# Roots and reciprocals of a two-layer kernel moved to a power operation on GpSimd

## The reference

```python
def _layernorm(x, axis=-1, eps=1e-05):
    m = jnp.mean(x, axis=axis, keepdims=True)
    v = jnp.var(x, axis=axis, keepdims=True)
    return (x - m) / jnp.sqrt(v + eps)
...
xn = _layernorm(x, axis=-1)
x = x + attention0(xn) + experts(xn)     # distance attention: softmax(-sqrt(d2)); 7 experts and a shared one
xn = _layernorm(x, axis=-1)
x = x + attention1(xn) + ffn1(xn)        # dot-product attention
# ffn1:
real = jnp.einsum('bti,io->bto', x, jnp.cos(theta + theta_noise))
imag = jnp.einsum('bti,io->bto', x, jnp.sin(phi + phi_noise))
return jnp.sqrt(real * real + imag * imag)
```

## Time and profile before

| | |
|---|---|
| time, median of 2 runs | 1760.43 us (1755.08 and 1765.78) |
| span of the profiled execution | 1763.0 us |
| PE / DVE / ACT / POOL busy | 84% / 79% / 88% / 18% of the span |

### The profile page before, as it was taken

How to read it: one execution, slowest core, us unless ns; L and a number is a source line. 1 busy time by engine, 2 the same in 40 slices (tenths; PEclk the granted TensorE clock), 3 DMA queues, 4 the chain that set the end, 5 groups by cost and what they waited for, 6 DMA issues and landing times. The chain is left out here.

```text
span 1763.0 us, 25680 instructions
## 1 busy us (share of the span) xinstructions
PE 1483.9 (84%) x8038; PEld 490.8 (28%) x8039; DVE 1387.5 (79%) x1687; ACT 1547.0 (88%) x959; POOL 323.9 (18%) x239
## 2 busy tenths in 40 slices
PE   5737988998898888878888887476699999999997
PEld 3411233233323332332333223354211111111113
DVE  6658966977887788779877975278699999999996
ACT  3537997999999999999999999254699999999996
POOL 2310660221122022202220221353300000000000
PEclk9755978999999999999999989778655555555556
DMA  6781231011101110111011100384300000000001
GB/s 199 209 247 36 67 110 34 27 27 35 28 26 35 30 34 25 35 30 34 25 30 35 31 22 12 63 198 155 100 27 27 27 26 23 27 27 27 27 22 48
DMA packets 80328, 99.07 MB, mean 56 GB/s; under 512 B 23874, under 2 KB 52690, under 8 KB 80290
## 3 DMA queue, kind: packets, MB, share of 16 engines
q1 hardware_dynamic: 72162, 78.23, 15.3%
q0 software_dynamic: 8128, 20.36, 4.2%
HBM read 52.69 MB, written 45.88 MB: 56 GB/s over the span
## 5 line engine op out<-in xcount | busy, mean ns | idle before, releaser
L1129 DVE TENSOR_SCALAR scores<-ring 128x1024 f32<-128x1024 f32 x512 | 597.7, 1214 | 59.2 <-PE ring L930 59.0
L1468 PE MATMUL a_ring<-a_stk 72*128 72x512 bf16 x1024 | 480.8, 621 | 6.5 <-DMA a_stk<-stack 6.5
L1604 DVE TENSOR_REDUCE a_den<-a_exp 128x2 f32<-128x2048 f32 x192 | 426.3, 2278 | 36.3 <-ACT a_exp L1579 36.3
L1419 ACT ACTIVATE scores<-scores 128x8192 f32<-128x8192 f32 x64 | 446.3, 7020 | 0.2
L1412 ACT ACTIVATE scores<-scores 128x8192 f32<-128x8192 f32 x60 | 417.6, 7022 | 16.8 <-DVE scores L1129 16.6
L1579 ACT ACTIVATE a_exp<-a_ring 128x1024 f32<-128x1024 f32 x384 | 428.0, 2133 | 3.5 <-PE a_ring L1468 3.5
L942 PE MATMUL pvb<-scores,val 128*9 128x256 f32 x4096 | 325.4, 395 | 48.4 <-ACT scores L1419 39.1
L930 PE MATMUL ring<-stk 72*128 72x512 bf16 x1024 | 333.0, 411 | 27.2 <-DMA w<-in_w 17.1
L1581 ACT ACTIVATE a_ring<-a_ring 128x1024 f32<-128x1024 f32 x128 | 203.0, 2144 | 0.0
L1468 PEld LDWEIGHTS a_ring<-a_stk 72*128 72x128 bf16 x1024 | 69.8, 111 | 416.8 <-ACT a_exp L1579 287.2
L1581 ACT ACTIVATION_READ_ACCUMULATOR a_ring<-a_ring 128x1 f32 x128 | 143.6, 1314 | 0.0
(11 more groups left out here) (181 smaller groups left out, 1151.0 us busy)
## 6 DMA issues: line engine op xcount, KB each, us to landing
stk<-stack SPq DMA_DIRECT2D x64, 192.0 KB
a_stk<-stack SPq DMA_DIRECT2D x64, 192.0 KB, 2.8
stack<-qp SPq DMA_DIRECT2D x8, 768.0 KB, 3.5
stack<-kp SPq DMA_DIRECT2D x8, 768.0 KB, 4.2
xj<-xg SPq DMA_DIRECT2D x16, 320.0 KB, 3.3
yg<-ht POOLq DMA_DIRECT2D x16, 320.0 KB, 3.1
stack<-qp SPq DMA_DIRECT2D x8, 512.0 KB, 4.5
stack<-kp SPq DMA_DIRECT2D x8, 512.0 KB, 4.9
```

The costliest lines, as they stand in the source:

```text
L1129: nc.vector.tensor_scalar(S[place][:, j * N:(j + 1) * N], tile[:], 1e-12, None, ALU.max).then_inc(ring_free, 1)
L1419: nc.scalar.activation(S[place][:], S[place][:], ACT.Exp, scale=-1.0).then_inc(exp_done, 1)
L1468: mm = nc.tensor.matmul(out[:, cols], stk[place][:, Q, i * P:(i + 1) * P], stk[place][:, K, cols], start=True, stop=True)
L1604: nc.vector.tensor_reduce(den[side][:, h, 2 * pair:2 * pair + 2], E[pair][:], axis=AX, op=ALU.add).then_inc(summed, 1)
```

## The change

Both roots leave ACT and the reciprocal leaves DVE. Two constants, -0.5 and 0.5, stand in a tile `powers`. POOL raises the variance plus eps (128 x 8) to the power -0.5 in one instruction, which gives the reciprocal of the deviation, and the sums of squares (128 x 1024) to the power 0.5, which gives the magnitudes. Both are tensor-tensor operations with the exponent broadcast as the second operand. The new POOL steps are `deviations(b)`, which waits for `var_ready`, and `magnitudes(b)`, which waits for `pow_ready`. SP's and PE's programs are the same as before.

```diff
+    R["powers"] = sb("powers", [P, 2])
...
+            chain.step(nc.vector.memset(R["powers"][:, 0:1], -0.5))
+            chain.step(nc.vector.memset(R["powers"][:, 1:2], 0.5))
...
-            def magnitudes(b):
-                act.wait_ge(pow_ready, b + 1)
-                nc.scalar.activation(mag[:, :, :], mag[:, :, :], ACT.Sqrt).then_inc(mag_ready, 1)
-
-            def begin(b):
-                if not first and is_first(b):
-                    keep_attention(b)
-                act.wait_ge(var_ready, b + 1)
-                nc.scalar.activation(rstd[:], mv[:, :, 1], ACT.Sqrt).then_inc(std_ready, 1)
...
-                if not is_first(b):
-                    keep_sums(b - 1) if first else magnitudes(b - 1)
+                if first and not is_first(b):
+                    keep_sums(b - 1)
...
-                if first and not is_last(b):
-                    begin(b + 1)
...
-                    if not is_last(b):
-                        begin(b + 1)
...
+            def deviations(b):
+
+                pool.wait_ge(var_ready, b + 1)
+                nc.gpsimd.tensor_tensor(rstd[:], mv[:, :, 1], R["powers"][:, 0:1].to_broadcast([P, NT]),
+                                        ALU.pow).then_inc(std_ready, 1)
+
+            def magnitudes(b):
+                pool.wait_ge(pow_ready, b + 1)
+                flat = mag[:, :, :].rearrange("p t c -> p (t c)")
+                nc.gpsimd.tensor_tensor(flat, flat, R["powers"][:, 1:2].to_broadcast([P, N]),
+                                        ALU.pow).then_inc(mag_ready, 1)
+
             def batch(b):
                 if not first and not is_last(b):
                     begin(b + 1)
+                if not first and not is_first(b):
+                    magnitudes(b - 1)
+                if first and not is_last(b):
+                    deviations(b + 1)
 
                 pool.wait_ge(kp_ready, b)
                 pool.wait_ge(qk_f, 2 * b + 2)
                 nc.gpsimd.tensor_tensor(kr[:], kf[:], kp[:, 0, :], ALU.subtract).then_inc(kr_ready, 1)
                 pool.wait_ge(kp1_ready, b + 1)
                 nc.gpsimd.tensor_tensor(kp[:, 2, :], kr[:], kp[:, 1, :], ALU.subtract).then_inc(kp_ready, 1)
+                if not first and not is_last(b):
+                    deviations(b + 1)
...
                 begin(0)
+                deviations(0)
                 for b in range(B):
                     batch(b)
+                magnitudes(B - 1)
...
-                begins.step(nc.vector.reciprocal(rstd[:], rstd[:]))
-                begins.wait()
```

More of the change, by code:

```diff
@@ L487, in batch @@
                                              ).then_inc(mix_out, 1)
-                    if not is_last(b):
-                        begin(b + 1)
-            each_batch(act, batch, begin)
-            keep_sums(B - 1) if first else magnitudes(B - 1)
+            if not first:
+                keep_attention(0)
+            each_batch(act, batch)
+            if first:
+                keep_sums(B - 1)
         @block.gpsimd
@@ L519, in _ @@
                 nc.gpsimd.memset(ones[:], 1.0).then_inc(made, 1)
-                each_batch(pool, batch)
+                each_batch(pool, batch, deviations)
             else:
                 begin(0)
+                deviations(0)
                 for b in range(B):
                     batch(b)
+                magnitudes(B - 1)
         @block.vector
@@ L532, in _ @@
             before = chain.count
-            BEGIN_STEPS, STEPS, SUM_STEPS = 3, 2, 3
+            BEGIN_STEPS, STEPS, SUM_STEPS = 2, 2, 3
             x_of = lambda b, t: X[:, bass.ds(b * NT + t, 1), :].rearrange("p o c -> p (o c)")
```

## The result

The changed kernel takes 2423.81 us against 1760.43: ratio 1.3768, 95% interval 1.371 to 1.3825. The range on record ended at 1863. Beside the kernel before on another chip, in a second comparison, the ratio was 1.3703 (1.3678 to 1.3729).

The account below looks back on a forecast made before the run. It took the order of waits in layer 1's `prepare`, not one engine's work, as the bound where the change acts. Four powers of 13.8 us less 13.7 gave +41.5 on 1760.4, so 1802 us; range 1765 to 1863.

Parts of the forecast that it names:

- the price p: Time of one POOL power over 128 x 1024 in layer 1's `prepare`; taken as 13.8 us, between 2.12 and 29.7.
- lower bound of 2.12 us: Least time for the large power: POOL's own pass over two operands of 1024 columns, 2.12 us.
- The chain: Layer 1's `prepare`: gathers wait for variances, `add_magnitudes` for POOL's large powers; four powers in sequence, moving layer 1 by 4p - 11.2.
- my sum for layer 1, 4p - 11.2: Predicted growth of layer 1's `prepare` in us, p being one large power's time; 3p - 2.2 for p under 9.
- my step: Predicted time of each event in layer 1's `prepare`, such as a split of q at 1192.2 + p.
- the small power: POOL's power over 128 x 8 replacing root and reciprocal: 0.5 us, an even exchange; bounds 0.1 and 2.1 us.
- my sum for 2.12 us: Rival of a cheap power hidden behind its operand reads: whole kernel +1.7, 1762 us; chance 0.14 near one pass.
- Layer 0: First `prepare`: second `normalise` no longer waits behind `qf` on ACT, q's stores leave 3.1 us earlier; gain 2.5 us.
- The table loads: Removed ACT loads of 1.28 us each, covered by idle time, costed at nothing; rival with them on the path: chance 0.02.
- the very dear power: Rival for the large power: from 29.7 us on, each step waiting for the one before; +105 and more, 1866 us; chance 0.12.
- the cheap ones: Rivals with a cheap large power: 2.12 us gives 1762 us, chance 0.14; up to 12.2 us, chance 0.27 (10.6 gives 1789).
- The chance of slower: Whole kernel slower by over 2%: 0.43 for p from 12.2 to 29.7 plus 0.12 for dearer, 0.55.

## Why the prediction was wrong, point by point

**The step that failed is the price p.** I took 13.8 us from ten DVE instructions of range reduction, and called 29.7 us, fourteen operations at a pass of 2.12 us each, an upper bound. The runs showed 163.2 us in its place, 5.5 times that bound. The count assumed that a power is as long as one chain of plain steps and that each step costs one pass over all 128 partitions; which of the two fails, and so why a power is this dear, stays open. Five widths show what it costs: 1.67 us at 8 columns (with the exponent -0.5), 41.1 at 256, 81.9 at 512, 122.7 at 768, 163.2 at 1024, which is 0.159 us a column ((163.24 - 81.94) / 512) and some 0.6 us besides (for 8 columns that would be 1.9). The multiplication in the power's place settles that it is the operation and not the operands, the broadcast or the waits. The exponent 2 at the same price fits one routine for all exponents. My lower bound of 2.12 us for a pass was not one either: the multiplication took 1.89.

The Trainium skill (GPSIMD Engine Reference, Elementwise — side-by-side cycle accounting), which I had cited with about 12 cycles per element for branching code, came to 10.2 us as I read it, and the power in the trace takes 16 times that; no run here shows that it is code of that kind. If the page's element is one partition's and a core works off its 16 partitions one after the other, the same figure is an estimated 192 cycles or 0.160 us a column at the 1.2 GHz that the page states, which agrees with the 0.159 measured. That the routine works so is not shown by any run here, and the section's other figures for GpSimd count a whole column as the element, so the second reading is a guess that fits one number.

**The chain held, its small terms did not.** With the measured p my sum for layer 1, 4p - 11.2, gives +641.8; measured +663.6. In us from POOL's first gather, my steps with p = 163.24 in them:

| event | before | my step | measured |
|---|---|---|---|
| second gathers begin | 12.1 | 22.0 | 23.4 |
| split of q, batch 0 | 31.7 | 36.6 | 43.1 |
| split of q, batch 1 | 60.8 | 223.0 | 234.3 |
| split of q, batch 2 | 81.2 | 408.6 | 427.3 |
| last `kr` | 106.9 | 586.7 | 606.2 |
| last `add_magnitudes` | 117.7 | 759.5 | 781.1 |

The missing 21.6 us are many small terms, read between the events of the table:

- 5.9 in the gathers: from the first issue of a group to the landing of its last rows it is 13.8, 14.5 and 14.5 us, where I took 12.3. In each group one issue takes 2.24 to 3.92 us in place of 0.95, while DVE is at two-operand additions.
- 4.2 in the small power: 1.64 to 1.68 us each, and 1.9 to 2.0 us from the variance to the next gather, where I took 0.5. It stands in the chain three times, not four as I wrote, so its bounds would move the sum by -1.2 and +4.8.
- 7.5 where DVE's additions start together with POOL's `kr`: the addition of `yro` 5.92 in place of 2.2, and the first two `add_magnitudes` 2.94 in place of 1.2.
- 2.0, net, from each split of q to the next variance (from that of batch 2 to the third power), with two casts of 2.50 us that I had counted as 0.69.
- 2.0 from the last `kr` to the last `add_magnitudes`, where the third `add_magnitudes` of 3.13 and a third cast of 2.50 stand: 11.5 us to the last sum of squares and not 9.6.

With a cheap power these terms would have been all of the result: my sum for 2.12 us was +1.7, and the multiplication with 1.89 us measured +24. I had named the slower DVE instructions as a risk of the forecast and priced them nowhere; the slower gathers I had not seen.

**Layer 0** was right in direction and mechanism: first phase 2.4 us shorter in the windows above against 2.5 predicted, and 0.9983 alone. The mechanism is in the changed trace: the cast of q in the first batch runs alone in 0.69 us, q's stores go out at 30.09 and not at 32.29, and the wait for the stores ends at 44.10 and not at 45.34.

```profile
28.11 0.69 DVE L627 CAST qp<-qr 128x1024 bf16<-128x1024 f32 x1
...
30.09 1.98 SPq L318 DMA_DIRECT2D stack<-qp  x3
...
44.10 1.11 ACT L460 ACTIVATE qp<-pQ,bq0s 128x1024 bf16<-128x1024 f32 x1 [6.79 <-DMA stack<-kp]
```

q's stores gained 2.2 us and not 3.1: 1.8 from the cast and 0.4 of the 1.3 that I took for DVE, since ACT wrote the first q part 0.9 us later than before (25.71 and not 24.81), behind a first small power of 1.66 us. At the wait for the stores the gain is 1.24 us, and the last stores to land there are k's in both traces. So that the phase as a whole came out 2.4 shorter is in part luck: among the traces with and without these powers the difference is between nothing and 2.4 us.

**The table loads** cost nothing, as taken. The price of 2.66 us a switch from the Trainium skill (ScalarE: Activation LUTs, What ACT_TABLE_LOAD costs) found no path to act on. **The rivals:** that of the very dear power had the right side and the chance of 0.12, but its time, 1866, came from the same false bound. None of the cheap ones happened. The chance of slower, 0.55, was held down by the belief that a known pass of POOL says something of an unknown operation on it.

## What to carry to other kernels

An operation that a trace does not show has no upper bound from its neighbours: here two operations of one instruction form, over the same tiles, took 1.89 and 163.24 us. Measure a new operation alone before its place in the order is argued about. And where an in-order queue both issues transfers and computes, a wait put ahead of the issues delays all that they feed: issuing gathers ahead of steps of 1.7 us was worth 19 us here, and keeping POOL's wait for their landing out of the way of its next step 10.5 (122.0 to 111.5).

## What the runs showed of the hardware that I had not expected

- A power on POOL costs 0.159 us a column of 128 partitions and some 0.6 us besides, the same for the exponents 0.5 and 2 (163.24 us for 1024 columns), where ACT takes the root of the same tile in 1.06 us.
- A DVE addition with two operands in SBUF that starts beside such a power is not held to the power's end: 82.4 us at 1024 columns (power 163.2), 82.0 at 768 (power 122.7), and no hold at 512 (power 81.9), where eight additions took 2.92 us.
- The same additions beside a POOL instruction of two microseconds take 5.9 us (beside `kr`) and 7.5 us (beside the multiplication and `kr`) in place of 2.2, when both start in the same moment.
- An issue of a gather by POOL takes 0.95 us, and up to 3.92 us where DVE is at two-operand additions.
- `attention0` was 22 to 33 us longer on most other chips, whatever kernel ran there (1026.1 us before, 1059.2 at most); why was not looked into.
